# Expert tiles of a mixture-of-experts stage taken in pairs, with the results folded by a product instead of transposed and added

## The chip, the cores and the metric

One core of one Trainium2 chip. The metric is the device time of one execution in microseconds (us); the kernel before has a median of 809.62 us over 3 runs (809.58 to 811.24). TensorE is the matrix engine, VectorE (DVE) and ScalarE (ACT) work elementwise, GpSimd (POOL) does here the scatters, SyncE (SP) issues loads. Matmuls read SBUF and write PSUM, which has eight banks of 128 x 512 fp32.

## The reference, cut to what matters

`x` is 32 x 64 x 16 x 16, that is 8192 tokens of 64 channels. A depthwise convolution and a hashed attention block come first; the change doesn't touch them. Then each token goes to two of eight experts, each a gated network with 682 hidden units:

```python
probs = softmax(flat @ router_w.T)
topk_probs, topk_idx = top_k(probs, 2)
topk_probs = topk_probs / (sum(topk_probs) + 1e-9)
h1 = einsum('nc,ehc->neh', flat, w1)
h3 = einsum('nc,ehc->neh', flat, w3)
y = einsum('neh,ech->nec', silu(h1) * h3, w2)
out = einsum('ne,nec->nc', gates, y)
```

The kernel computes only the two experts chosen for a token. All of it is in fp32.

## The kernel before, in words

**First part (to about 430 us).** Eight groups of four images run through a software pipeline. At its end each token's normalised row, its gate and its destination are scattered to HBM (`expert_rows`), sorted by expert, and a small schedule says for each of NT = 71 tiles of MT = 256 rows which expert and which rows it has. An expert row holds the 64 values twice, then the gate, then the place of the result.

**The expert loop (437 to 783 us)** is what the change touches. A tile goes through these steps, each on the engine named; the order of each engine's work is written out by hand, and semaphores tie the engines together.

- SP, `load_weights(t)` (L382 to L386): 576 KB of the expert's weights into one of 4 slots, after `down` of tile t-4. `load_rows(t)` (L388 to L392): 256 rows into one of 8 slots of `xin`, after the scatter of tile t-8, which reads that slot. SP issues them in turn (L402 to L405): weights of t, rows of t+3, weights of t+1. A wait for one holds up all that follow.
- TensorE, `turn_rows(t)` (L731): two 128x128 transposes of the rows into the PSUM view `xt_ps`, which shares a bank with `h1_ps[0]`. ScalarE copies it into `xs` (`store_xs`, L917).
- TensorE, `up(t, q)`, q = 0 to 2 (L738): 8 products of 64 x 128 weights with 256 tokens; w1 lies on the upper 64 partitions and w3 on the lower. Each q fills a bank `h1_ps[q]` and a bank `h3_ps[q]`.
- ScalarE takes silu of `h1_ps[q]` (L933), VectorE multiplies it with `h3_ps[q]` into `units` (`gated`, L1250 to L1256).
- TensorE, `down(t)` (L752): 12 products of 128 x 64 weights with 256 tokens, accumulated in one bank, even chunks on partitions 0 to 63 and odd ones on 64 to 127. So the bank holds two half sums. ScalarE copies it into `ysb` (`store_results`, L922).
- TensorE, `turn_results(t)` (L762): two 128x128 transposes of `ysb` into the other half of the bank. A row then has the two half sums side by side.
- VectorE, `gate_out(t)` (L1258 to L1268): copies one half, adds the other, multiplies by the gate into `yout`: three passes over 128x128.
- GpSimd, L514 to L522: two indirect scatters of 128 rows into `expert_results`.

TensorE's order (L768 to L780) is up(t), turn_rows(t+1), turn_results(t-2), down(t-1). ScalarE's (L927 to L938) is three silus, store_xs(t+1), store_results(t-1). VectorE's (L1270 to L1276) is three gated units, gate_out(t-2).

**After the loop** SP and ScalarE read both results of every token back, VectorE adds them and the residual, and ScalarE stores the output.

Of the kernel before, what the change touches and what calls it, by code (L numbers as in the profile page):

```python
# [6 lines left out]
P = 128  # L7
B, C, HH, WW = 32, 64, 16, 16
# [14 lines left out]
MT = 256  # L23
REG = T + MT
NT = (2 * T + NE * (MT - 1)) // MT
ROW = 2 * C + 2
ROW_SLOTS = 3
DUMP = 2 * T
# [14 lines left out]

CONSTS = dict(ident=P, pair_mean=P, before=P, ones=P, descend=BUCKETS, head_of=HEADS, v_mask=2 * C,
              v_heads=2 * HEADS, region=NE * NJ, scan_keep=NE * (NJ + 1), k_rows=T // MT, tile_no=1, tile_at=1,
              pad=2 * ROW, q_one=1, k_one=1)
SMALLS = dict(bias2=1, g1=1, b1=1, g2=1, b2=1, fc1_bias0=2, proj=C + M + 2 * C, fc1=DFF, fc2=2 * C, fc2_bias=C,
              router=NE)

# [13 lines left out]
def hybrid_block(nc, x, consts, smalls, weights, out):  # L63
    with ExitStack() as ctx:
# [15 lines left out]
        def const_of(name, p=P):  # L80
            return const[0:p, CONST_AT[name][0]:CONST_AT[name][1]]
# [14 lines left out]
        k_rows = const_of("k_rows")  # L96
        tile_no = const_of("tile_no")
        tile_at = const_of("tile_at")
        pad = const_of("pad").rearrange("p (h w) -> p h w", h=2)
        bias2 = small_of("bias2")  # L100
        g1 = small_of("g1", C)
# [108 lines left out]

        xin = sb("xin", [P, X_SLOTS, 2, ROW])
        wbuf = sb("wbuf", [P, W_SLOTS, CH * P + CH * C])
        xs = sb("xs", [P, 2, MT])
        silu = sb("silu", [P, NU, 512])
        units = sb("units", [P, 2, NU, 512])
        ysb = sb("ysb", [P, 2, MT])
        ysum = sb("ysum", [P, 2, 2, C])
        yout = sb("yout", [P, X_SLOTS, 2, C])
        res = srow[:, :, :, :, :].rearrange("p g k j w -> p (g k j w)")[:, 0:RES_SLOTS * 2 * NJ * C]\
            .rearrange("p (b k j c) -> p b k j c", b=RES_SLOTS, k=2, c=C)  # L220
# [23 lines left out]

        h1_ps = [bk12[:, 0, :], bk12[:, 1, :], bk34[:, 0, :]]
        h3_ps = [bk34[:, 1, :], bk5[:, :], bk6]
        xt_ps = h1_ps[0][:, 0:MT]
        yt_banks = [bk0, bk7]

        waited = sem("waited")  # L250
        consts_loaded = sem("consts_loaded")
# [93 lines left out]
        down_done = sem("down_done")  # L345
        ysb_ready = sem("ysb_ready")
        y_turned = sem("y_turned")
        ysum_ready = sem("ysum_ready")
        yout_ready = sem("yout_ready")
        res_loaded = [sem(f"res_loaded{b}") for b in range(RES_SLOTS)]  # L350
        t3_sum = sem("t3_sum")
# [64 lines left out]
        def _(pool):  # L416
# [95 lines left out]
            pipeline(iteration)  # L512

            for t in range(NT):  # L514
                pool.wait_ge(yout_ready, t + 1)
                pool.sem_inc(waited, 1)
                for h in range(2):
                    g.indirect_dma_start(  # L518
                        results[:, :],
                        bass.IndirectOffsetOnAxis(ap=xin[:, t % X_SLOTS, h, ROW - 1:ROW].bitcast(U32), axis=0),  # L520
                        yout[:, t % X_SLOTS, h, :], None, bounds_check=DUMP - 1, oob_is_err=False)\
                        .then_inc(y_scattered[t % X_SLOTS], 16)  # L522

        @block.tensor
        def _(pe):
# [204 lines left out]

            def turn_rows(t):  # L731
                pe.wait_ge(xin_loaded[t % X_SLOTS], 16 * (t // X_SLOTS + 1))
                wait(pe, silu_ready, NU * (t - 1) + 1)
                for h in range(2):
                    last = turn(xt_ps[:, h * P:(h + 1) * P], xin[:, t % X_SLOTS, h, 0:2 * C], ident)  # L735
                last.then_inc(xt_turned, 1)

            def up(t, q):  # L738
                if q == 0:
                    pe.wait_ge(xs_ready, t + 1)  # L740
                    pe.wait_ge(w_loaded[t % W_SLOTS], 16 * (t // W_SLOTS + 1))
                wait(pe, unit_ready, NU * (t - 1) + q + 1)
                for ch in range(2):
                    at = (2 * q + ch) * P
                    for half, bank in ((0, h1_ps[q]), (1, h3_ps[q])):
                        part = slice(half * C, (half + 1) * C)
                        last = mm(bank[:, ch * MT:(ch + 1) * MT], wbuf[part, t % W_SLOTS, at:at + P],  # L747
                                  xs[part, t % 2, :], start=True, stop=True)
                        if ch == 1:
                            last.then_inc((h1_ready, h3_ready)[half], 1)  # L750

            def down(t):  # L752
                wait(pe, yout_ready, t - 1)
                pe.wait_ge(unit_ready, NU * (t + 1))
                for q in range(NU):
                    for ch in range(2):
                        at = W2_AT + (2 * q + ch) * C
                        last = mm(yt_banks[t % 2][ch * C:(ch + 1) * C, 0:MT], wbuf[:, t % W_SLOTS, at:at + C],  # L758
                                  units[:, t % 2, q, ch * MT:(ch + 1) * MT], start=q == 0, stop=q == NU - 1)
                last.then_inc(down_done, 1)  # L760

            def turn_results(t):  # L762
                pe.wait_ge(ysb_ready, t + 1)
                for h in range(2):
                    last = turn(yt_banks[t % 2][:, MT + h * P:MT + (h + 1) * P], ysb[:, t % 2, h * P:(h + 1) * P], ident)  # L765
                last.then_inc(y_turned, 1)

            turn_rows(0)  # L768
            for t in range(NT):
                for q in range(NU):  # L770
                    up(t, q)
                if t + 1 < NT:
                    turn_rows(t + 1)
                if t > 1:
                    turn_results(t - 2)
                if t > 0:
                    down(t - 1)
            turn_results(NT - 2)
            down(NT - 1)
            turn_results(NT - 1)  # L780

        @block.scalar
        def _(act):
# [130 lines left out]
            for e in range(NE // 2, NE):  # L914
                write_pad(act, act.value_load(pad_row[0:1, e:e + 1], min_val=0, max_val=NE * REG - MT))

            def store_xs(t):  # L917
                act.wait_ge(xt_turned, t + 1)
                wait(act, h3_ready, NU * (t - 1))
                f(xs[:, t % 2, :], xt_ps, ACT.Copy).then_inc(xs_ready, 1)  # L920

            def store_results(t):  # L922
                act.wait_ge(down_done, t + 1)
                wait(act, y_turned, t - 1)
                f(ysb[:, t % 2, :], yt_banks[t % 2][:, 0:MT], ACT.Copy).then_inc(ysb_ready, 1)  # L925

            store_xs(0)  # L927
            for t in range(NT):
                for q in range(NU):
                    n = NU * t + q  # L930
                    act.wait_ge(h1_ready, n + 1)
                    wait(act, unit_ready, n - NU + 1)
                    f(silu[:, q, :], h1_ps[q], ACT.Silu).then_inc(silu_ready, 1)  # L933
                if t + 1 < NT:
                    store_xs(t + 1)
                if t > 0:
                    store_results(t - 1)
            store_results(NT - 1)  # L938

            for b in range(X_SLOTS):  # L940
                act.wait_ge(y_scattered[b], 32 * ((NT - b + X_SLOTS - 1) // X_SLOTS))
# [19 lines left out]
        def _(dve):  # L961
# [293 lines left out]
                    wait(dve, down_done, t - 1)  # L1255
                tt(units[:, t % 2, q, :], h3_ps[q], silu[:, q, :], ALU.mult).then_inc(unit_ready, 1)  # L1256

            def gate_out(t):  # L1258
                dve.wait_ge(y_turned, t + 1)
                halves = yt_banks[t % 2][:, MT:2 * MT].rearrange("p (h a c) -> p h a c", h=2, a=2)  # L1260
                v.tensor_copy(ysum[:, t % 2, :, :], halves[:, :, 0, :]).then_inc(ysum_ready, 1)
                dve.wait_ge(ysum_ready, 2 * t + 1)
                tt(ysum[:, t % 2, :, :], halves[:, :, 1, :], ysum[:, t % 2, :, :], ALU.add).then_inc(ysum_ready, 1)
                dve.wait_ge(ysum_ready, 2 * t + 2)
                dve.wait_ge(xin_loaded[t % X_SLOTS], 16 * (t // X_SLOTS + 1))
                wait(dve, y_scattered[t % X_SLOTS], 32 * (t // X_SLOTS))
                tt(yout[:, t % X_SLOTS, :, :], ysum[:, t % 2, :, :],  # L1267
                   wide(xin[:, t % X_SLOTS, :, 2 * C], C), ALU.mult).then_inc(yout_ready, 1)  # L1268

            for t in range(NT):  # L1270
                for q in range(NU):
                    gated(t, q)
                if t > 1:
                    gate_out(t - 2)
            gate_out(NT - 2)
            gate_out(NT - 1)  # L1276

            for i in range(NG):
                dve.wait_ge(res_loaded[i % RES_SLOTS], 32 * (i // RES_SLOTS + 1))
# [5 lines left out]


DVE_SETUP = 2


def wait(engine, semaphore, value):  # L1290
# [18 lines left out]
def constants():  # L1309
    import numpy as np  # L1310

    p = np.arange(P)[:, None]
    n = np.arange(P)[None, :]
    h = np.arange(HEADS)
    t = {name: np.zeros((P, wide), np.float32) for name, wide in CONSTS.items()}
    t["ident"][:] = p == n
    t["pair_mean"][:] = 0.5 * (p // 2 == n // 2)
    t["before"][:] = p < n
    t["ones"][:] = 1.0
    t["descend"][:] = BUCKETS - np.arange(BUCKETS)  # L1320
    t["head_of"][:] = (p // DH == h) | (p >= C)
    head = np.arange(2)[None, :, None] * 4 + p[:, :, None] // M
    t["v_mask"][:] = (head == np.arange(C)[None, None, :] // DH).reshape(P, -1)
    t["v_heads"][:] = (head == h[None, None, :]).reshape(P, -1)
    t["region"][:] = np.repeat(np.arange(NE) * REG, NJ)
    t["scan_keep"][:] = np.tile(np.arange(NJ + 1) > 0, NE)
    t["k_rows"][:] = np.arange(T // MT) * MT
    t["tile_no"][:] = p
    t["tile_at"][:] = p * MT
    pad = np.zeros((P, 2, ROW), np.float32)  # L1330
    pad[:, :, ROW - 1] = np.full((P, 2), DUMP, np.uint32).view(np.float32)
    t["pad"][:] = pad.reshape(P, -1)
    t["q_one"][C] = 1.0
    t["k_one"][C + 1] = 1.0
    return np.concatenate([t[name] for name in CONSTS], axis=1)

# [56 lines left out]
```

## Time and profile before

| | |
|---|---|
| median of 3 runs | 809.62 us (809.58 to 811.24) |
| span of the profiled execution | 809.8 us |
| TensorE busy, weight loads apart | 664.6 us (82%) |
| VectorE, ScalarE, GpSimd busy | 462.7, 354.0, 370.7 us |
| first `up` of the expert loop, first `up` of its last tile | 437.22, 775.10 us |
| results read back from | 789.75 us |

The profiled execution's own time is its span, 809.8 us. The profile is of one execution. Starts of instructions are recorded; ends of matmuls are modelled, so that matmuls seem to overlap. PE is TensorE's matmuls, PEld its weight loads. An entry in brackets says how long an engine was idle before an instruction and what released it. An SPq row is the issue of a transfer by SP, not the transfer.

### The profile page before, as it was taken

Reading aid. Unit: us, or ns where it says so; the run is one execution under the profiler, and the core shown is the slowest. Engines: PE = TensorE matmul, PEld = TensorE weight load, DVE = VectorE, ACT = ScalarE, POOL = GpSimd, SP = SyncE. Lnnn points to the kernel's source line nnn. Section 1 sums busy time; section 2 is a strip of 40 time slices with the busy share of each in tenths; the row PEclk is TensorE's granted clock in tenths of the full one; section 3 lists DMA queues with packets and bytes.
Section 4 is the critical chain, followed back from the end, with each engine's and each line's share of the span. In section 5 each row is a group of like instructions: output and inputs, shape, how many; then the busy total and the mean of one; then the engine's idle time right before and its main releaser. Section 6 shows DMA issues by size and latency. Waiting matters only on the chain.

```text
span 809.8 us, 13968 instructions
## 1 busy us (share of the span) xinstructions
PE 664.6 (82%) x4632; PEld 502.3 (62%) x4632; DVE 462.7 (57%) x1094; ACT 354.0 (44%) x693; POOL 370.7 (46%) x377
## 2 busy tenths in 40 slices
PE   2598989797989797886404999999999999999960
PEld 1476768586867576673303777777777777777740
DVE  2256677677777777633311565566655666555645
ACT  1142737373737373523202544555445554455520
POOL 2203241767676768726662233443334433344440
PEclk9665868677777878555556999999999999999985
DMA  2000000010101010101183455556555555555508
GB/s 82 2 14 1 14 0 15 16 51 17 50 18 37 18 37 17 47 7 40 36 194 96 136 168 158 155 157 164 175 169 160 155 160 161 174 167 167 171 9 311
DMA packets 46615, 75.47 MB, mean 93 GB/s; under 512 B 7488, under 2 KB 30048, under 8 KB 46544
## 3 DMA queue, kind: packets, MB, share of 16 engines
q1 hardware_dynamic: 34512, 57.12, 24.2%
q0 software_dynamic: 8640, 12.74, 4.8%
q10 hardware_dynamic: 3392, 4.73, 1.8%
q8 instruction: 37, 0.61, 0.3%
q14 instruction: 34, 0.28, 0.1%
HBM read 58.54 MB, written 16.47 MB: 93 GB/s over the span
## 4 chain that ended last, share of the span: by engine, by line
PE 49%; POOL 23%; issue 17%; DVE 6%; DMA 3%; ACT 1%; POOLq 0%; SPq 0%; ACTq 0%; DVEq 0%
PE bk L747 25%; POOL expert_rows L496 15%; PE bk L758 12%; PE bk L735 3%; POOL rr L451 3%; PE bk L765 2%; DMA srow<-expert_results 2%; POOL r L462 2%; PE bk L553 1%; POOL x2t L480 1%; POOL r L457 1%; PE bk L577 1%; PE bk L570 1%; PE bk L638 1%; DMA small<-in_smalls 1%
## 5 line engine op out<-in xcount | busy, mean ns | idle before, releaser
L1256 DVE TENSOR_TENSOR units<-bk,silu 128x512 f32<-128x512 f32 x213 | 147.4, 692 | 164.7 <-ACT silu L933 164.7
L518 POOL DMA_INDIRECT expert_results<-yout,xin x142 | 139.5, 983 | 217.2 <-DVE yout L1267 190.4
L747 PE MATMUL bk<-xs,wbuf 64*128 64x256 f32 x1704 | 204.4, 386 | 1.2 <-ACT xs L920 1.1
L747 PEld LDWEIGHTS bk<-xs,wbuf 64*128 64x128 f32 x1704 | 160.0, 188 | 44.3 <-issue 26.7
L933 ACT ACTIVATE silu<-bk 128x512 f32<-128x512 f32 x213 | 127.2, 597 | 86.1 <-PE bk L747 86.1
L496 POOL DMA_INDIRECT expert_rows<-srow,pos x128 | 131.3, 1026 | 44.2 <-issue 38.0
L758 PE MATMUL bk<-units,wbuf 128*64 128x256 f32 x852 | 107.6, 388 | 0.0
L758 PEld LDWEIGHTS bk<-units,wbuf 128*64 128x64 f32 x852 | 54.8, 136 | 32.4 <-issue 11.7
L925 ACT ACTIVATE ysb<-bk 128x256 f32<-128x256 f32 x71 | 27.3, 384 | 84.2 <-PE bk L758 84.2
L451 POOL TENSOR_TENSOR rr<-vare,c_mhalf 128x16 f32<-128x16 f32 x8 | 23.4, 2923 | 79.3 <-DVE vare L1036 79.3
L735 PE MATMUL bk<-const,xin 128*128 128x128 f32 x142 | 31.3, 302 | 29.2 <-DMA xin<-expert_rows 29.2
L735 PEld LDWEIGHTS bk<-const,xin 128*128 128x128 f32 x142 | 14.3, 141 | 52.5 <-issue 52.5
L920 ACT ACTIVATE xs<-bk 128x256 f32<-128x256 f32 x71 | 26.9, 378 | 34.7 <-PE bk L735 34.7
L638 PEld LDWEIGHTS bk<-vblk,prob_t 128*128 128x128 f32 x256 | 34.8, 218 | 6.6 <-ACT prob_t L845 4.8
L665 PEld LDWEIGHTS bk<-small,hid 128*128 128x128 f32 x256 | 35.8, 227 | 1.8 <-ACT hid L861 1.8
L638 PE MATMUL bk<-vblk,prob_t 128*128 128x72 f32 x256 | 36.8, 305 | 0.0
L613 PE MATMUL bk<-kblk,qt 65*128 65x256 f32 x128 | 36.8, 425 | 0.0
L665 PE MATMUL bk<-small,hid 128*128 128x64 f32 x256 | 36.5, 311 | 0.2 <-ACT hid L861 0.2
L553 PE MATMUL bk<-const,hsum 128*128 128x128 f32 x192 | 36.5, 344 | 0.0
L1086 DVE TENSOR_REDUCE smax<-bk 128x16 f32<-128x512 f32 x32 | 21.8, 681 | 25.7 <-PE bk L613 25.5
L838 ACT ACTIVATE prob<-ssub 128x512 f32<-128x512 f32 x32 | 19.4, 626 | 37.3 <-DVE ssub L1088 37.2
L553 PEld LDWEIGHTS bk<-const,hsum 128*128 128x128 f32 x192 | 34.2, 262 | 0.0
(184 smaller groups left out, 981.5 us busy)
## 6 DMA issues: line engine op xcount, KB each, us to landing
wbuf<-in_weights SPq DMA_DIRECT2D x71, 576.0 KB, 4.0
xin<-expert_rows SPq DMA_DIRECT2D x71, 130.0 KB, 2.3
expert_results<-yout,xin POOLq DMA_INDIRECT x142, 2.8
xg<-in_x SPq DMA_DIRECT2D x8, 256.0 KB, 2.8
expert_rows<-srow,pos POOLq DMA_INDIRECT x128, 2.4
srow<-expert_results SPq DMA_DIRECT2D x8, 256.0 KB, 5.6
srow<-expert_results ACTq DMA_DIRECT2D x8, 256.0 KB, 6.4
out<-hid ACTq DMA_DIRECT2D x8, 256.0 KB, 5.8
```

Source lines behind the costliest of these rows:

```text
L451: g.tensor_tensor(rr[:, :, :].rearrange("p a j -> p (a j)"), vare1[:, :, :].rearrange("p a j -> p (a j)"), c_mhalf[:, :], ALU.pow).then_in ...
L496: g.indirect_dma_start(rows[0:NE * REG, :], bass.IndirectOffsetOnAxis(ap=pos[:, d, k, j:j + 1], axis=0), srow[:, d % ROW_SLOTS, k, j, :], ...
L518: g.indirect_dma_start(results[:, :], bass.IndirectOffsetOnAxis(ap=xin[:, t % X_SLOTS, h, ROW - 1:ROW].bitcast(U32), axis=0), yout[:, t % ...
L553: last = mm(o, hsum[:, s, h0 + dy:h0 + dy + 8, :], ident, start=False, stop=dy == 2)
L613: last = mm(bk12[:, p % 2, bp * 256:(bp + 1) * 256], qt[:, j * P:(j + 1) * P], kblk[:, m, :, :].rearrange("c h m -> c (h m)"), start=True, ...
L638: last = mm(av_ps[:, 2 * (p % 2) + bp, :], prob_t[:, p % 2, 2 * bp + ch, :], vblk[:, m, ch, :], start=ch == 0, stop=ch == 1)
L665: last = mm(y_ps[:, 2 * q + par, :], hid[:, a, par, q * P:(q + 1) * P], fc2_s[:, a, :], start=a == 0, stop=a == 1)
L735: last = turn(xt_ps[:, h * P:(h + 1) * P], xin[:, t % X_SLOTS, h, 0:2 * C], ident)
L747: last = mm(bank[:, ch * MT:(ch + 1) * MT], wbuf[part, t % W_SLOTS, at:at + P], xs[part, t % 2, :], start=True, stop=True)
L758: last = mm(yt_banks[t % 2][ch * C:(ch + 1) * C, 0:MT], wbuf[:, t % W_SLOTS, at:at + C], units[:, t % 2, q, ch * MT:(ch + 1) * MT], start= ...
L933: f(silu[:, q, :], h1_ps[q], ACT.Silu).then_inc(silu_ready, 1)
L1256: tt(units[:, t % 2, q, :], h3_ps[q], silu[:, q, :], ALU.mult).then_inc(unit_ready, 1)
```

## The change

The loop runs over NPAIR = 36 pairs of tiles; the last pair has tile 70 alone. TensorE's order for pair i is: up of both tiles (six groups of 8 products), row turns of pair i+1, folds of pair i-1, then down of both tiles of pair i. `xs` holds both tiles of a pair side by side and is filled by one copy of 512 columns; the turned rows fill the whole bank `h1_ps[0]`.

The result turn becomes `fold_results`: a product whose stationary operand is `ysb` (128 x 128) and whose moving operand is a constant 128 x 64 matrix `fold`, two 64 x 64 identities on top of each other. It turns the results and adds the two half sums at once. The folds of a pair fill 4 x 64 = 256 columns of the bank `h3_ps[0]`. `gate_out` is then one multiplication over 128 x 256 for a pair, from PSUM to `yout`. `down` accumulates in a bank of its own for each tile of a pair. SP's order and the slots stay; GpSimd's scatters of both tiles wait for the pair's `gate_out`.

```diff
@@ constants
-              pad=2 * ROW, q_one=1, k_one=1)
+              pad=2 * ROW, q_one=1, k_one=1, fold=C)
+    t["fold"][:] = p % C == np.arange(C)[None, :]
@@ tiles
-        xs = sb("xs", [P, 2, MT])
+        xs = sb("xs", [P, 2 * MT])
-        xt_ps = h1_ps[0][:, 0:MT]
-        yt_banks = [bk0, bk7]
+        xt_ps = h1_ps[0]
+        fold_ps = h3_ps[0]
+        y_banks = [bk0, bk7]
@@ GpSimd
             for t in range(NT):
-                pool.wait_ge(yout_ready, t + 1)
+                pool.wait_ge(yout_ready, t // 2 + 1)
@@ TensorE
             def turn_rows(t):
                 pe.wait_ge(xin_loaded[t % X_SLOTS], 16 * (t // X_SLOTS + 1))
-                wait(pe, silu_ready, NU * (t - 1) + 1)
+                wait(pe, silu_ready, NU * (t - 1 - t % 2) + 1)
...
             def up(t, q):
                 if q == 0:
-                    pe.wait_ge(xs_ready, t + 1)
+                    pe.wait_ge(xs_ready, t // 2 + 1)
                     pe.wait_ge(w_loaded[t % W_SLOTS], 16 * (t // W_SLOTS + 1))
+                    wait(pe, yout_ready, t // 2 - 1)
                 wait(pe, unit_ready, NU * (t - 1) + q + 1)
...
             def down(t):
-                wait(pe, yout_ready, t - 1)
+                wait(pe, ysb_ready, t - 1)
                 pe.wait_ge(unit_ready, NU * (t + 1))
...
-            def turn_results(t):
+            def fold_results(t):
                 pe.wait_ge(ysb_ready, t + 1)
+                wait(pe, yout_ready, t // 2)
+                wait(pe, unit_ready, NU * min(2 * (t // 2) + 3, NT - 1) + 1)
                 for h in range(2):
-                    last = turn(yt_banks[t % 2][:, MT + h * P:MT + (h + 1) * P], ysb[:, t % 2, h * P:(h + 1) * P], ident)
+                    at = (2 * (t % 2) + h) * C
+                    last = mm(fold_ps[:, at:at + C], ysb[:, t % 2, h * P:(h + 1) * P], fold, start=True, stop=True)
                 last.then_inc(y_turned, 1)
 
-            turn_rows(0)
-            for t in range(NT):
-                for q in range(NU):
-                    up(t, q)
-                if t + 1 < NT:
-                    turn_rows(t + 1)
-                if t > 1:
-                    turn_results(t - 2)
-                if t > 0:
-                    down(t - 1)
-            turn_results(NT - 2)
-            down(NT - 1)
-            turn_results(NT - 1)
+            for t in range(2):
+                turn_rows(t)
+            for i in range(NPAIR):
+                for t in pair(i):
+                    for q in range(NU):
+                        up(t, q)
+                if i + 1 < NPAIR:
+                    for t in pair(i + 1):
+                        turn_rows(t)
+                if i > 0:
+                    for t in pair(i - 1):
+                        fold_results(t)
+                for t in pair(i):
+                    down(t)
+            for t in pair(NPAIR - 1):
+                fold_results(t)
@@ ScalarE
+            def store_xs(i):
+                n = len(pair(i))
+                act.wait_ge(xt_turned, 2 * i + n)
+                wait(act, h3_ready, NU * 2 * i)
+                f(xs[:, 0:n * MT], xt_ps[:, 0:n * MT], ACT.Copy).then_inc(xs_ready, 1)
...
+            for i in range(NPAIR):
+                for t in pair(i):
+                    for q in range(NU):
...
+                if i + 1 < NPAIR:
+                    store_xs(i + 1)
+                for t in pair(i):
+                    store_results(t)
@@ VectorE
+            def gate_out(i):
+                n = len(pair(i))
+                dve.wait_ge(y_turned, 2 * i + n)
+                for t in pair(i):
+                    dve.wait_ge(xin_loaded[t % X_SLOTS], 16 * (t // X_SLOTS + 1))
+                    wait(dve, y_scattered[t % X_SLOTS], 32 * (t // X_SLOTS))
+                at = 2 * i % X_SLOTS
+                tt(yout[:, at:at + n, :, :], fold_ps[:, 0:2 * n * C].rearrange("p (t h c) -> p t h c", t=n, h=2),
+                   xin[:, at:at + n, :, 2 * C].unsqueeze(3).broadcast_to([P, n, 2, C]), ALU.mult).then_inc(yout_ready, 1)
+
+            for i in range(NPAIR):
+                for t in pair(i):
+                    for q in range(NU):
+                        gated(t, q)
+                if i > 0:
+                    gate_out(i - 1)
+            gate_out(NPAIR - 1)
+
+def pair(i):
+    return range(2 * i, min(2 * i + 2, NT))
```

## Rows read from the trace of the kernel before

**Rows 1.** Busy time by stretch: stretch, length, engines (instructions), TensorE clock, DMA.

```profile
600.00:620.00 20.00, 20.00 (x168) 14.16 (x168) 12.13 (x26) 10.01 (x21) 7.86 (x8) 1.00 0.57 167
```

**Rows 2.** Timeline of TensorE over one tile: start, us, line, operation, [idle before].

```profile
606.08 2.86 PE L747 MATMUL bk<-xs,wbuf 64*128 64x256 f32 x24
...
608.88 0.44 PE L735 MATMUL bk<-const,xin 128*128 128x128 f32 x2
...
609.15 0.38 PE L765 MATMUL bk<-const,ysb 128*128 128x128 f32 x2
...
609.46 1.52 PE L758 MATMUL bk<-units,wbuf 128*64 128x256 f32 x12
...
610.91 2.86 PE L747 MATMUL bk<-xs,wbuf 64*128 64x256 f32 x24
```

**Rows 3.** Products of `up` and `down`: count, ns least/median/most, first and last start.

```profile
L747 PE MATMUL bk<-xs,wbuf x1704: 376/376/790, 437.2 to 777.6; 64*128 64x256 f32 x190
...
L758 PE MATMUL bk<-units,wbuf x852: 379/379/431, 445.5 to 781.8; 128*64 128x256 f32 x171
```

**Rows 4.** Waits of SP's queue, 460 to 760 us: total, times, longest.

```profile
SPq L390 <- DMA expert_results<-yout,xin: 154.2, 56, 5.2
```

**Rows 5.** Timeline of TensorE in the first part: fc2, then transposes.

```profile
99.59 3.73 PE L665 MATMUL bk<-small,hid 128*128 128x64 f32 x32
103.15 1.04 PE L625 MATMUL bk<-const,prob 128*128 128x128 f32 x8
```

**Rows 6.** Timeline of VectorE and GpSimd beside the tile of rows 2.

```profile
607.88 0.69 DVE L1256 TENSOR_TENSOR units<-bk,silu 128x512 f32<-128x512 f32 x1 [1.55 <-ACT silu L933]
...
610.85 0.29 DVE L1267 TENSOR_TENSOR yout<-ysum,xin 128x128 f32<-128x128 f32 x1
...
612.00 0.98 POOL L518 DMA_INDIRECT expert_results<-yout,xin  x1 [2.55 <-DVE yout L1267]
...
613.28 0.98 POOL L518 DMA_INDIRECT expert_results<-yout,xin  x1 [0.30 <-issue]
```

**Rows 7.** Timeline of the loop's head: row loads, first copy, first and third `up`.

```profile
433.90 6.58 SPq L391 DMA_DIRECT2D xin<-expert_rows  x6
...
436.78 0.38 ACT L920 ACTIVATE xs<-bk 128x256 f32<-128x256 f32 x1 [34.69 <-PE bk L735]
...
437.22 4.13 PE L747 MATMUL bk<-xs,wbuf 64*128 64x256 f32 x24 [0.47 <-ACT xs L920]
...
446.92 2.86 PE L747 MATMUL bk<-xs,wbuf 64*128 64x256 f32 x24
```

**Rows 8.** Timeline of a tile's second scatter and of SP's issues after it.

```profile
574.70 0.98 POOL L518 DMA_INDIRECT expert_results<-yout,xin  x1 [0.30 <-issue]
...
580.66 0.38 SPq L391 DMA_DIRECT2D xin<-expert_rows  x1
...
603.64 0.98 POOL L518 DMA_INDIRECT expert_results<-yout,xin  x1 [0.30 <-issue]
...
608.38 0.38 SPq L391 DMA_DIRECT2D xin<-expert_rows  x1
...
609.54 0.35 SPq L385 DMA_DIRECT2D wbuf<-in_weights  x1
...
622.93 0.98 POOL L518 DMA_INDIRECT expert_results<-yout,xin  x1 [0.30 <-issue]
...
625.88 0.38 SPq L391 DMA_DIRECT2D xin<-expert_rows  x1
```

**Rows 9.** Issue to landing, 460 to 760 us: weights first, then the scatters.

```profile
DMA to landing us min/median/max: 3.4/4.0/5.4
...
DMA to landing us min/median/max: 2.1/2.9/5.2
```

**Rows 10.** Timeline of the loop's end: last `up`, read-back.

```profile
775.10 2.86 PE L747 MATMUL bk<-xs,wbuf 64*128 64x256 f32 x24
...
789.75 9.04 SPq L412 DMA_DIRECT2D srow<-expert_results  x8
```

More of the change, by code:

```diff
@@ L25 @@
 NT = (2 * T + NE * (MT - 1)) // MT
+NPAIR = (NT + 1) // 2
 ROW = 2 * C + 2
@@ L98, in hybrid_block @@
         tile_at = const_of("tile_at")
+        fold = const_of("fold")
         pad = const_of("pad").rearrange("p (h w) -> p h w", h=2)
@@ L216, in hybrid_block @@
         ysb = sb("ysb", [P, 2, MT])
-        ysum = sb("ysum", [P, 2, 2, C])
         yout = sb("yout", [P, X_SLOTS, 2, C])
@@ L347, in hybrid_block @@
         y_turned = sem("y_turned")
-        ysum_ready = sem("ysum_ready")
         yout_ready = sem("yout_ready")
@@ L732, in turn_rows @@
                 pe.wait_ge(xin_loaded[t % X_SLOTS], 16 * (t // X_SLOTS + 1))
-                wait(pe, silu_ready, NU * (t - 1) + 1)
+                wait(pe, silu_ready, NU * (t - 1 - t % 2) + 1)
                 for h in range(2):
-                    last = turn(xt_ps[:, h * P:(h + 1) * P], xin[:, t % X_SLOTS, h, 0:2 * C], ident)
+                    last = turn(xt_ps[:, (2 * (t % 2) + h) * P:(2 * (t % 2) + h + 1) * P], xin[:, t % X_SLOTS, h, 0:2 * C], ident)
                 last.then_inc(xt_turned, 1)
@@ L747, in up @@
                         last = mm(bank[:, ch * MT:(ch + 1) * MT], wbuf[part, t % W_SLOTS, at:at + P],
-                                  xs[part, t % 2, :], start=True, stop=True)
+                                  xs[part, t % 2 * MT:(t % 2 + 1) * MT], start=True, stop=True)
                         if ch == 1:
@@ L757, in down @@
                         at = W2_AT + (2 * q + ch) * C
-                        last = mm(yt_banks[t % 2][ch * C:(ch + 1) * C, 0:MT], wbuf[:, t % W_SLOTS, at:at + C],
+                        last = mm(y_banks[t % 2][ch * C:(ch + 1) * C, 0:MT], wbuf[:, t % W_SLOTS, at:at + C],
                                   units[:, t % 2, q, ch * MT:(ch + 1) * MT], start=q == 0, stop=q == NU - 1)
                 last.then_inc(down_done, 1)
-            def turn_results(t):
+            def fold_results(t):
                 pe.wait_ge(ysb_ready, t + 1)
+                wait(pe, yout_ready, t // 2)
+                wait(pe, unit_ready, NU * min(2 * (t // 2) + 3, NT - 1) + 1)
                 for h in range(2):
-                    last = turn(yt_banks[t % 2][:, MT + h * P:MT + (h + 1) * P], ysb[:, t % 2, h * P:(h + 1) * P], ident)
+                    at = (2 * (t % 2) + h) * C
+                    last = mm(fold_ps[:, at:at + C], ysb[:, t % 2, h * P:(h + 1) * P], fold, start=True, stop=True)
                 last.then_inc(y_turned, 1)
-            turn_rows(0)
-            for t in range(NT):
-                for q in range(NU):
-                    up(t, q)
-                if t + 1 < NT:
-                    turn_rows(t + 1)
-                if t > 1:
-                    turn_results(t - 2)
-                if t > 0:
-                    down(t - 1)
-            turn_results(NT - 2)
-            down(NT - 1)
-            turn_results(NT - 1)
+            for t in range(2):
[14 more added lines that the diff above has]
+                fold_results(t)
         @block.scalar
@@ L915, in _ @@
                 write_pad(act, act.value_load(pad_row[0:1, e:e + 1], min_val=0, max_val=NE * REG - MT))
[L917 to L920, printed above, removed]
+            def store_xs(i):
[3 more added lines that the diff above has]
+                f(xs[:, 0:n * MT], xt_ps[:, 0:n * MT], ACT.Copy).then_inc(xs_ready, 1)
             def store_results(t):
@@ L924, in store_results @@
                 wait(act, y_turned, t - 1)
-                f(ysb[:, t % 2, :], yt_banks[t % 2][:, 0:MT], ACT.Copy).then_inc(ysb_ready, 1)
+                f(ysb[:, t % 2, :], y_banks[t % 2][:, 0:MT], ACT.Copy).then_inc(ysb_ready, 1)
             store_xs(0)
[L928 to L938, printed above, removed]
+            for i in range(NPAIR):
+                for t in pair(i):
+                    for q in range(NU):
+                        n = NU * t + q
+                        act.wait_ge(h1_ready, n + 1)
+                        wait(act, unit_ready, n - NU + 1)
+                        f(silu[:, q, :], h1_ps[q], ACT.Silu).then_inc(silu_ready, 1)
+                if i + 1 < NPAIR:
+                    store_xs(i + 1)
+                for t in pair(i):
+                    store_results(t)
             for b in range(X_SLOTS):
@@ L1256, in gated @@
                 tt(units[:, t % 2, q, :], h3_ps[q], silu[:, q, :], ALU.mult).then_inc(unit_ready, 1)
[L1258 to L1276, printed above, removed]
+            def gate_out(i):
[14 more added lines that the diff above has]
+            gate_out(NPAIR - 1)
             for i in range(NG):
```

## The prediction

> **What bounds the kernel now.** The views were read from the coarse to the fine. The chain of work that ended last gives the time between 437 and 783 us to the lines of the expert loop, nearly all TensorE's; the change touches that loop alone (and 64 columns of constants). The busy time by stretch shows TensorE at 20.00 of 20 us, clock 1.00, so 2.4 GHz, while VectorE has 12.1, ScalarE 10.0 and GpSimd 7.9 [rows 1]. Then the timeline of one tile, from start to start, since ends of matmuls are modelled [rows 2]: `up` (24 products) begins at 606.08, the two row turns at 608.88, the two result turns at 609.15, `down` (12 products) at 609.46, the next `up` at 610.91. A tile takes 4.83 us.
>
> Inside `up` the starts are (2.86 - 0.376)/23 = 0.108 us apart (a product is shown with 0.376, the median of its line [rows 3]), inside `down` (1.52 - 0.379)/11 = 0.104; two turns begin (0.38 - 0.27) = 0.11 apart, a turn being shown with about 0.27. So the last `up` product starts at 608.56, and the turn only 0.32 later; from the last `down` product (610.60) to the next `up` it is 0.31; from turns to `down` 0.20; from turn to turn of the other kind 0.16. The reader should see that a change of the kind of product costs about 0.2 us over the pace inside a kind, four kinds to a tile.
>
> The other thing to see is off TensorE. SP issues in order: rows of t+3, weights of t+1, rows of t+4. The rows wait for the scatter of the tile eight earlier, 154 us in 56 waits, up to 5.2 [rows 4]. Weights queue behind that wait. Today it costs nothing; by how much, is worked out below.
>
> **The change, for a pair of tiles.** Call S the start of a pair's first `up`.
> 1. Kinds of product: 48 `up` products, 4 row turns, 4 folds, 24 `down` products, so four changes of kind where two tiles have eight. 47 x 0.108 + 0.32 + 3 x 0.11 + 0.16 + 3 x 0.112 + 0.20 + 23 x 0.104 + 0.31 = 9.12 us, against 2 x 4.83 = 9.65 measured: 0.53 less.
> 2. Folds. A fold is a true fp32 product with 128 stationary columns and 64 moving ones, in place of a transpose. This kernel has such products in fc2: 32 in 3.73 us, so (3.73 - 0.27)/31 = 0.112 each; and 8 transposes right behind them, (1.04 - 0.27)/7 = 0.11 [rows 5]. The fold costs nothing more; the transposes of this stretch keep the pace of those in the expert loop, so the clock is the same. The Trainium skill (TensorE: Matmul & The Clock Gate, Terms) calls transpose mode four times faster for fp32; by that the sum would be 843 (rival C), and the rows of fc2 disagree.
> 3. New waits on TensorE. Second `up` needs the first tile's products gated bank by bank. The first gated unit starts at S + 1.80 and takes 0.69 [rows 6], so it is done at S + 2.49; a release takes 0.06 (ScalarE ends at 437.16, TensorE starts at 437.22 [rows 7]): S + 2.55. TensorE gets there at S + 24 x 0.108 = 2.59. The product just fits, but its weight load, which runs ahead, does not. Bounds: 0, and 0.2 us a pair, the price of a change of kind, where the loads are not hidden either; nothing is gained by a wait. I take the middle, 0.1, so 9.22. The second `down` needs the last gated unit: units come 8 x 0.108 = 0.86 apart, the sixth ends at S + 1.80 + 5 x 0.86 + 0.69 = 6.8; `down` gets there at S + 7.7. Next `up` writes the bank of the folds and waits for the gating of the pair before, done at S + 7.3 of the earlier pair: 1.8 us to spare. Turns wait for a silu done 0.6 us before.
> 4. VectorE: three passes of 0.29 a tile become one of 128x256 a pair, between 0.29 (128x128) and 0.69 (128x512), linear 0.43. VectorE is not the bound; gain 0. It moves the output: folds end at S + 6.5, the pass waits in order for the sixth gated unit and ends at S + 7.3.
> 5. ScalarE: one copy of 512 columns for two of 256, ready at about S + 6.8, needed at S + 9.1: 0. The result copies now follow each `down`; the next silu is due 1.1 us after the next `up` starts, and a copy takes 0.4: 0.
> 6. GpSimd and SP. Today the first scatter starts 0.86 after yout (611.14 to 612.00) and the second 1.28 later [rows 6]. Now both tiles' yout come at once, so four follow each other: starts S + 8.15, 9.44, 10.7, 12.0. Nobody waits for GpSimd but SP. From the start of a tile's second scatter to SP's issue of the rows it frees I read D = 2.95 (622.93 to 625.88), 4.74 (603.64 to 608.38) and, the longest found, 5.96 (574.70 to 580.66); weights are issued 1.16 later (608.38 to 609.54) [rows 8] and land after 4.0 (3.4 to 5.4) [rows 9]. So the weights of the pair two ahead land at S + 9.44 + D + 1.16 + 4.0 = S + 14.6 + D, and are needed at S + 2 x 9.12 = 18.2. D may be 3.6. Today the same sum is 7.2 + D + 5.16 against 4 x 4.83 = 19.3: D may be 6.9, which no row reaches. The change eats 3.3 us of that margin. Which D will hold? My guess is that the long ones have weights in flight beside them. If so, by the schedule above the earlier pair's second weight load is issued at about S + 7 and lands at S + 11 to 11.7; the second scatter sends its data from S + 10.4, so it meets the tail of it only: D about 3.2 to 3.7. A longer pair would thin the traffic. So the loop lies near the limit, and I take it as costing nothing on the mean, with 9.4 as its upper bound (D = 4.2).
> The page DMA: Bandwidth & Descriptors of the Trainium skill (the fit under its fixed cost) gives 2.0 us plus bytes over 436 GB/s for a software DMA. A scatter of 32 KB would land in 2.1 us by it, D near 2.9, and this limit would never bite; the trace has 2.1 as the least, 2.9 as the median and 5.2 as the most [rows 9].
> 7. Head. The first `up` now waits for the rows of tile 1 too. Six row loads are issued in 6.58 us, 1.24 apart; so `up` begins near 438.5 in place of 437.22 [rows 7]. The low clock of the first products cost it 1.27 (4.13 for 2.86); I take 1.7, since TensorE has done less before it. 438.5 + 47 x 0.108 + 1.7 + 0.32 + 0.33 + 0.2 + 2.4 + 0.31 puts pair 1 at 448.9, where tile 2 began at 446.92: +2.0 us.
> 8. Tail. Tile 70 stands alone. Today SP reads the results back 14.65 us after its `up` (775.10 to 789.75), by six scatters at the end that wait in GpSimd's line [rows 10]. Now six scatters again, the first at S + 5.5: 5.5 + 6 x 1.29 + 1.0 = S + 14.3: -0.35.
> 9. Constants grow from about 0.56 to 0.59 MB, 0.1 us at most: 0.
>
> **The sum.** Pair 35 starts at 448.9 + 34 x 9.22 = 762.4, against 775.10: -12.7; tail -0.35; -13.0 in all. The profiled execution's span is 809.8, the median 809.62, 0.02% apart. 809.6 - 13.0 = 796.6. With 9.12: 793.2. With 9.40: 802.7. About 0.2%, 1.6 us, is what a measurement here can tell from no change.
>
> **Rivals.**
> A. The forecast, 0.70: TensorE stays the bound, 9.12 to 9.4 us a pair. For: full busy time now, other engines at 60% or less, the 0.3 us at each change of kind.
> B. Weights late, the rival on the slow side: SP issues them behind the rows, rows behind the later, bunched scatters. The pair takes (14.6 + D)/2. It decides from D = 3.6; at D = 4.4 it is 9.5 and the time 806; the gain is gone at 9.60, D = 4.6; at D = 5 it is 9.8 and the time 816; at 5.96, 832. For it: two of the three D read are over 4.6. Against: the guess of step 6, by which the second scatter meets the end of a weight transfer only. Partly so (gain left, up to 808): 0.12. Equal: 0.03. Slower, about 816: 0.11.
> C. The fold is dear: if a true fp32 product is four passes of the array where a transpose is one, it takes 4 x 0.11 = 0.44, and 142 of them add 142 x 0.33 = 47 us: 843. The fc2 rows stand against it: 0.02. (It is the Trainium skill's rule of step 2.)
> D. The change does not do what it says: at each place where a change of kind goes, TensorE waits for a gated unit instead. Should the second `up` wait 0.5 us a pair, the time is 809. That step 3 leaves only 0.04 us of room is for it, the bound of 0.2 there against: 0.02.
>
> **How the numbers follow.** The likeliest case is A, 796.6. Chances: faster A and the partial B, 0.82; same 0.03 + 0.02 = 0.05; slower 0.11 + 0.02 = 0.13. The range goes down to 790.5 (9.05 a pair, should one of the changes of kind left be cheaper than today, and pair 1 a microsecond earlier) and up to 806.5 (B with D = 4.4).
>
> **What would show it.** In steady state: 48 `up` products in one run of starts 0.108 apart, at the most a gap of 0.1 at the 25th; folds 0.11 apart; pairs 9.2 apart; TensorE with next to no idle on a DMA. Rival B would show as TensorE idle before `up`, released by DMA wbuf, and D over 4. Rival C as folds 0.4 apart. The forecast is wrong if pairs are over 9.45 or under 9.05 apart, or if the head costs over 3 us.

## The result, and the profile after

The changed kernel takes 814.06 us (median of 20 runs, 810.9 to 817.71) against 810.15 us of the kernel before in the same runs (808.24 to 813.04): a ratio of 1.0043, 95% interval 1.003 to 1.0056. It is slower by 3.5 us by that ratio, 3.9 by the medians, where 13 us less was forecast. The profiled execution has a span of 811.5 us and a time of 813.63. In every run with both numbers on record the time is 1.7 to 2.2 us over the span; the text ahead of the prediction takes the profiled execution of the kernel before to have its span, 809.8 us, as its time, which leaves these 2 us out. The difference that was forecast doesn't hang on it.

TensorE's timeline of one pair in steady state, kernel after (start, us, operation):

```profile
603.12 5.49 PE L749 MATMUL bk<-xs,wbuf 64*128 64x256 f32 x48
...
608.54 0.66 PE L736 MATMUL bk<-const,xin 128*128 128x128 f32 x4
...
609.03 1.00 PE L770 MATMUL bk<-const,ysb 128*128 128x64 f32 x8
...
609.97 2.81 PE L760 MATMUL bk<-units,wbuf 128*64 128x256 f32 x24
...
612.71 5.49 PE L749 MATMUL bk<-xs,wbuf 64*128 64x256 f32 x48
```

A pair takes 9.59 us, against 9.65 for two tiles before [rows 2]. Start to start: `up` 5.42, turns 0.49, folds 0.94, `down` 2.74. The line of the folds is the one to look at. The code calls for four products in a pair and the row says x8. The view of that line says the same for the whole run: 142 calls, 284 matmuls. The first fence is of the kernel after (count, ns least/median/most, first and last start), the second has the result turns of the kernel before, 142 calls and 142 matmuls:

```profile
L770 PEld LDWEIGHTS bk<-const,ysb x284: 186/192/192, 454.5 to 783.8; 128*128 128x128 f32 x142
L770 PE MATMUL bk<-const,ysb x284: 222/275/323, 454.6 to 783.9; 128*128 128x64 f32 x142
```

```profile
L765 PEld LDWEIGHTS bk<-const,ysb x142: 137/141/143, 449.9 to 782.7; 128*128 128x128 f32 x142
L765 PE MATMUL bk<-const,ysb x142: 272/273/329, 450.0 to 782.8; 128*128 128x128 f32 x142
```

The stretch that answers to [rows 1] shows TensorE full as before and VectorE relieved, 9.83 of 20 us for 12.13:

```profile
600.00:620.00 20.00, 20.00 (x176) 15.94 (x177) 9.83 (x16) 10.14 (x19) 7.86 (x8) 1.00 0.59 183
```

Not every pair is steady. Here a pair's weights are late, those of its first tile a little and those of its second more (timeline of GpSimd, SP's issues and TensorE, kernel after):

```profile
525.43 0.98 POOL L519 DMA_INDIRECT expert_results<-yout,xin  x1 [0.30 <-issue]
...
530.18 0.38 SPq L392 DMA_DIRECT2D xin<-expert_rows  x1
531.35 0.35 SPq L386 DMA_DIRECT2D wbuf<-in_weights  x1
...
533.67 0.35 SPq L386 DMA_DIRECT2D wbuf<-in_weights  x1
...
535.32 2.86 PE L749 MATMUL bk<-xs,wbuf 64*128 64x256 f32 x24
...
538.39 2.86 PE L749 MATMUL bk<-xs,wbuf 64*128 64x256 f32 x24 [0.21 <-DMA wbuf<-in_weights]
```

The second scatter of a tile starts at 525.43, SP issues the rows it frees 4.75 us later, the weights behind them at 531.35 and 533.67. The pair before began at 525.50, so the first `up` comes 9.82 after it in place of 9.59, 0.23 late. The second starts at 538.39, 3.07 after the first, in place of 2.69, its distance in 30 of the 34 full pairs from pair 1 on (a little more than 24 x 0.109, since the starts inside `up` come in twos, some 0.01 to 0.04 us apart, and from two to two it is 0.216). The views of waits of TensorE and of SP, 460 to 770 us, kernel after:

```profile
PE bk L749 <- DMA wbuf<-in_weights: 0.9, 2, 0.7
```

```profile
SPq L391 <- DMA expert_results<-yout,xin: 165.7, 43, 9.6
```

SP's longest wait went from 5.2 [rows 4] to 9.6 us, but that one stands where the loop fills, from 450.9 to 461.2 us; from 470 us on the longest is 5.9. The sum of TensorE's waits by name (0.9) understates the cost, since idle time counts only from the modelled end of the last matmul (535.32 + 2.86 = 538.18, so 0.21 above, where by the starts 0.38 was lost); by starts, pairs 1 to 35 span 777.17 - 448.72 = 328.45 us where 33 x 9.59 and a last 9.38 make 325.85. So 2.6 us of this trace are weights that came late.

More than half of them follow one late scatter. GpSimd then idles 1.97 us in place of 0.30 before it, put down to "issue"; what that is, no run shows. Timeline of GpSimd and of TensorE, kernel after:

```profile
729.65 0.98 POOL L519 DMA_INDIRECT expert_results<-yout,xin  x1 [1.97 <-issue]
...
741.65 2.86 PE L749 MATMUL bk<-xs,wbuf 64*128 64x256 f32 x24 [0.68 <-DMA wbuf<-in_weights]
```

The two pairs around it take 10.07 and 10.50 us in place of 9.59, 1.4 us of the 2.6. Such a pause stands in the other traces too: in experiment 3 at 727.22, where no pair is longer for it, and in the kernel before at 725.89, where the weights of tile 62, issued at 732.91, make a tile of 5.01 us (731.49 to 736.50) in place of 4.83.

**The balance of the two traces**, from SP's first row load to the read-back: before 433.90 to 789.75, 355.85; after 432.95 to 791.30, 358.35; 2.5 more. Head, to the start of tile 2: 13.0, then 15.8: +2.75. Tiles 2 to 70: 328.2, then 328.45: +0.3, made of -2.3 (pairs at 9.59 and a last of 9.38) and +2.6 (late weights). Tail: 14.65, then 14.13: -0.5. The medians stand 3.9 apart; the other 1.4 is within the scatter of single runs.

### The profile page after: what moved, and what is told of

It reads as the page before. It is cut to its first block, busy times and chain, and to the rows that moved or that the text cites. A ratio compares the mean times of both kernels' runs of the same rounds, so it can differ in the third digit from the quotient of the medians.

```text
span 811.5 us, 14139 instructions
## 1 busy us (share of the span) xinstructions
PE 664.7 (82%) x4774; PEld 531.7 (66%) x4774; DVE 422.1 (52%) x917; ACT 355.6 (44%) x658; POOL 371.0 (46%) x377
## 4 chain that ended last, share of the span: by engine, by line
PE 47%; POOL 23%; issue 17%; DVE 6%; DMA 5%; ACT 1%; SPq 1%; POOLq 0%; ACTq 0%; DVEq 0%
PE bk L749 23%; POOL expert_rows L497 15%; PE bk L760 11%; PE bk L770 3%; POOL rr L452 3%; PE bk L736 3%; POOL r L463 2%; PE bk L554 1%; DMA wbuf<-in_weights 1%; POOL x2t L481 1%; POOL r L458 1%; PE bk L578 1%; PE bk L571 1%; DMA out<-hid 1%; DMA srow<-expert_results 1%
## 5 line engine op out<-in xcount | busy, mean ns | idle before, releaser
L749 PE MATMUL bk<-xs,wbuf 64*128 64x256 f32 x1704 | 198.0, 385 | 2.3 <-DMA wbuf<-in_weights 0.9
L749 PEld LDWEIGHTS bk<-xs,wbuf 64*128 64x128 f32 x1704 | 167.5, 188 | 32.5 <-issue 16.6
L760 PE MATMUL bk<-units,wbuf 128*64 128x256 f32 x852 | 99.9, 383 | 0.5 <-DVE units L1265 0.5
L760 PEld LDWEIGHTS bk<-units,wbuf 128*64 128x64 f32 x852 | 58.3, 137 | 28.3 <-issue 0.6
L736 PE MATMUL bk<-const,xin 128*128 128x128 f32 x142 | 24.1, 291 | 29.9 <-DMA xin<-expert_rows 29.9
L929 ACT ACTIVATE xs<-bk 128x512 f32<-128x512 f32 (+1 forms) x36 | 21.3, 591 | 36.9 <-PE bk L736 36.0
L666 PEld LDWEIGHTS bk<-small,hid 128*128 128x128 f32 x256 | 35.8, 227 | 1.8 <-ACT hid L869 1.8
L666 PE MATMUL bk<-small,hid 128*128 128x64 f32 x256 | 36.5, 311 | 0.2 <-ACT hid L869 0.2
L770 PE MATMUL bk<-const,ysb 128*128 128x64 f32 x284 | 35.9, 269 | 0.5 <-ACT ysb L934 0.5
L770 PEld LDWEIGHTS bk<-const,ysb 128*128 128x128 f32 x284 | 34.5, 192 | 1.3 <-ACT ysb L934 0.9
```

The source lines that it names most:

```text
L666: last = mm(y_ps[:, 2 * q + par, :], hid[:, a, par, q * P:(q + 1) * P], fc2_s[:, a, :], start=a == 0, stop=a == 1)
L736: last = turn(xt_ps[:, (2 * (t % 2) + h) * P:(2 * (t % 2) + h + 1) * P], xin[:, t % X_SLOTS, h, 0:2 * C], ident)
L760: last = mm(y_banks[t % 2][ch * C:(ch + 1) * C, 0:MT], wbuf[:, t % W_SLOTS, at:at + C], units[:, t % 2, q, ch * MT:(ch + 1) * MT], start=q ...
L770: last = mm(fold_ps[:, at:at + C], ysb[:, t % 2, h * P:(h + 1) * P], fold, start=True, stop=True)
```

## The experiments

Theory F: a plain fp32 product goes to TensorE as two matmuls of about 0.11 us and a transpose as one, so the folds cost 0.4 us a pair, and the pairing itself saves what was forecast. Theory W: weights are late behind the bunched scatters, through SP's order. The main rival, K: changes of kind are not what pairs save. All variants with pairs are edits of the changed kernel. Each run stood beside runs of the kernel before on the same chip; 811.28 us (first four) and 811.19 us (last four) were its medians.

**1. Pairs, with transposes in place of folds.**

```diff
...
-                    at = (2 * (t % 2) + h) * C
-                    last = mm(fold_ps[:, at:at + C], ysb[:, t % 2, h * P:(h + 1) * P], fold, start=True, stop=True)
+                    at = (2 * (t % 2) + h) * P
+                    last = turn(fold_ps[:, at:at + P], ysb[:, t % 2, h * P:(h + 1) * P], ident)
@@ gate_out
+                halves = fold_ps[:, 0:2 * n * P].rearrange("p (h a c) -> p h a c", h=2 * n, a=2)
+                v.tensor_copy(ysum[:, 0:2 * n, :], halves[:, :, 0, :]).then_inc(ysum_ready, 1)
+                dve.wait_ge(ysum_ready, 2 * i + 1)
+                tt(ysum[:, 0:2 * n, :], halves[:, :, 1, :], ysum[:, 0:2 * n, :], ALU.add).then_inc(ysum_ready, 1)
+                dve.wait_ge(ysum_ready, 2 * i + 2)
...
```

The part left out makes the tile `ysum` and its semaphore, and multiplies `ysum` by the gate in place of the folds.

> Pairs as in the change, but the results turned by transposes and the halves added by VectorE as before (three passes over 128x256). Theory F (a fold takes two matmuls of 0.112 us, a transpose one, and the pairing itself works): TensorE's work of a pair falls from 9.59 to 9.14 us. VectorE's three passes put the scatters 0.85 us later, so the weights of the pair two ahead land at S + 15.45 + D, with D about 3.5 as in the kernel after, which allows 9.48 a pair: 809 to 811 us, with TensorE waiting for wbuf in most pairs. Rival K (changes of kind are not what pairs save, and the fold costs nothing): pairs stay at 9.59 or more, 814 us or more. Rival N (weights never late for long): 9.14 a pair, 798 us.

Measured: 818.99 us, ratio 1.011 (1.007 to 1.015), slower than both kernels. TensorE's work fell as Theory F says; the weights ate it all. Timeline of TensorE and of SP's weight issues:

```profile
601.51 0.35 SPq L388 DMA_DIRECT2D wbuf<-in_weights  x1
...
602.80 2.86 PE L751 MATMUL bk<-xs,wbuf 64*128 64x256 f32 x24
...
605.81 2.86 PE L751 MATMUL bk<-xs,wbuf 64*128 64x256 f32 x24
...
611.23 0.35 SPq L388 DMA_DIRECT2D wbuf<-in_weights  x1
...
612.36 2.86 PE L751 MATMUL bk<-xs,wbuf 64*128 64x256 f32 x24
...
615.80 2.86 PE L751 MATMUL bk<-xs,wbuf 64*128 64x256 f32 x24 [0.58 <-DVE units L1267]
```

The second `up` comes 3.01 and 3.44 after the first, in place of 2.69. At 615.80 the view names VectorE as the releaser; but the gated unit that is waited for ends at 614.85 (614.16 + 0.69). The weights issued at 611.23 have a landing of their own in the view of transfers, 4.5 us later, at 615.7:

```profile
wbuf<-in_weights SPq DMA_DIRECT2D x1, 576.0 KB, 4.5
```

So this wait is put down to the wrong engine, and is one for weights. Pairs 1 to 35 span 780.68 - 446.80 = 333.9 us; experiment 7, in which no pair waits, has 312.15 for them: 22 us of waiting, 15 before the second `up` of a pair and 7 before the first. Expected was 809 to 811; the sign of the mechanism was right, its size was not.

**2. The same, with SP's rows two tiles ahead of the weights in place of three.** No weight load then stands behind the newest scatter.

```diff
-            for t in range(X_SLOTS - 2):
+            for t in range(X_SLOTS - 3):
                 load_rows(t)
...
-                if t + X_SLOTS - 1 - W_SLOTS < NT:
-                    load_rows(t + X_SLOTS - 1 - W_SLOTS)
+                if t + X_SLOTS - 2 - W_SLOTS < NT:
+                    load_rows(t + X_SLOTS - 2 - W_SLOTS)
```

> The same, and SP loads rows two tiles ahead of the weights in place of three, so that no weight load stands behind a late scatter. Theory F: 9.14 us a pair, no wait for wbuf, 814 - 15.3 - 2.5 = 796 us. Rival K: 811 to 814 us, 9.59 a pair.

Measured: 801.13 us, ratio 0.9871 (0.9847 to 0.9894). 18 us less than experiment 1, by the order of SP's loads alone. 796 was expected. A pair without a wait takes 9.19 us where 9.14 was expected, 1.7 us in 34; and pairs 1 to 35 take 764.66 - 449.54 = 315.1, 3.0 over the 312.15 of experiment 7. Two waits are put down to wbuf, 2.0 us together, so the order with rows two ahead doesn't end them all.

**3. The kernel of the change with that order of loads.** The same edit on the fold.

> The kernel of the change, with SP's rows two tiles ahead of the weights. Theory W (of the distance to the kernel before, 2.5 us are weights late now and then): every pair 9.59, no wait for wbuf, 811.5 us, about the time of before. Rival: the rows, not the weights, come late or nothing changes, 814 us.

Measured: 810.23 us, ratio 0.9991 (0.9974 to 1.0008), no wait for wbuf, and pairs 1 to 35 in 773.35 - 447.50 = 325.85 us, to the hundredth the 33 x 9.59 + 9.38 without a wait. The interval does not touch that of the change (1.003 to 1.0056). So late weights are most or all of what makes the change slower than before. Theory W holds, with one reserve: by the times the order of loads is worth 4 us here, by the trace 2.6, and experiment 6 leaves room for some 1 us that has nothing to do with pairs.

**4. Tile by tile, with the fold.** The kernel before, with only the product and VectorE's single pass (its edit is left out).

```diff
-                    last = turn(yt_banks[t % 2][:, MT + h * P:MT + (h + 1) * P], ysb[:, t % 2, h * P:(h + 1) * P], ident)
+                    last = mm(yt_banks[t % 2][:, MT + h * C:MT + (h + 1) * C], ysb[:, t % 2, h * P:(h + 1) * P], fold,
+                              start=True, stop=True)
...
```

> The kernel before, tile by tile, with the fold in place of the result transposes and of the two VectorE passes. Theory F: a tile takes 4.83 + 2 x 0.112 = 5.05 us, 810.2 + 71 x 0.224 = 826 us. Rival K (the fold costs what a transpose does): 810 us.

Measured: 822.13 us, ratio 1.0135 (1.0106 to 1.0164). TensorE's timeline of one tile, to be laid beside [rows 2]:

```profile
601.32 2.86 PE L748 MATMUL bk<-xs,wbuf 64*128 64x256 f32 x24
604.12 0.44 PE L736 MATMUL bk<-const,xin 128*128 128x128 f32 x2
604.39 0.56 PE L766 MATMUL bk<-const,ysb 128*128 128x64 f32 x4
604.88 1.52 PE L759 MATMUL bk<-units,wbuf 128*64 128x256 f32 x12
606.32 0.92 PE L748 MATMUL bk<-xs,wbuf 64*128 64x256 f32 x6
```

From the fold to `down` it is 0.49 in place of 0.31: a tile takes 5.00 us, 0.18 more, where 0.22 and 826 us were expected. From tile 2 to tile 70 this trace has 339.9 us against 328.2 before, 11.7 more, and behind the last `up` 0.7 less; 11 were measured. The fold alone is a loss.

**5. Plain product or stacked identity?** Experiment 2 with the result turns as plain products with the full identity, 128 moving columns; not one other instruction differs.

```diff
-                    last = turn(fold_ps[:, at:at + P], ysb[:, t % 2, h * P:(h + 1) * P], ident)
+                    last = mm(fold_ps[:, at:at + P], ysb[:, t % 2, h * P:(h + 1) * P], ident, start=True, stop=True)
```

> As pair_turn_rows2, but the four result turns of a pair are plain products with the full identity (128 moving columns) in place of transposes. Nothing else differs: same columns, same three VectorE passes, same SP order. Theory F (a plain fp32 product goes as two matmuls where a transpose goes as one, whatever its columns): 8 matmuls in place of 4, a pair 9.19 + 0.4 = 9.59 to 9.63 us, 801.1 + 14 = 815 us. Rival C (it was the stacked identity, or its 64 columns): 9.19 a pair, 801 us.

Measured: 814.08 us, ratio 1.0034 (1.0018 to 1.0051), 13 us over experiment 2. Pairs take 9.65 us. Its timeline, and that of experiment 7 (transposes) under it:

```profile
610.25 0.66 PE L738 MATMUL bk<-const,xin 128*128 128x128 f32 x4
610.74 1.06 PE L772 MATMUL bk<-const,ysb 128*128 128x128 f32 x8
611.73 2.81 PE L762 MATMUL bk<-units,wbuf 128*64 128x256 f32 x24
```

```profile
611.51 0.66 PE L738 MATMUL bk<-const,xin 128*128 128x128 f32 x4
612.00 0.60 PE L772 MATMUL bk<-const,ysb 128*128 128x128 f32 x4
612.53 2.81 PE L762 MATMUL bk<-units,wbuf 128*64 128x256 f32 x24
```

x8 and 0.99 us for the same four turns that are x4 and 0.53 as transposes. A call costs (1.06 - 0.275)/7 x 2 = 0.22 us as a plain product and (0.60 - 0.27)/3 = 0.11 as a transpose. It is the kind of product and not the shape: with half the columns the folds take 0.94, hardly less. No pair waits here, while experiment 2 has its 3.0 us of waits; so 34 x 0.46 = 15.6 less 3.0 is what the times should show, and 13 is what they show.

**6. The kernel before with rows two ahead.**

> The kernel before, with SP's rows two tiles ahead of the weights in place of three. Theory W (there the weights land long before they are needed): no change, 811 us. Rival (the order of the loads is worth something by itself): 1 us or more faster.

Measured: 809.67 us, ratio 0.9986 (0.9972 to 1.0001). That lies between theory (no change) and rival (1 us or more), and the interval, 2.3 us less to none, decides for neither; in the trace of the kernel before late weights cost 0.2 us, at one tile. The order of loads is worth 18 us to the pairs with transposes and 2 us at most to single tiles; it costs nothing there.

**7. Experiment 2 with rows one tile ahead of the weights** (`X_SLOTS - 4` and `X_SLOTS - 3 - W_SLOTS` in the edit of experiment 2).

> As pair_turn_rows2, rows one tile ahead of the weights. Theory W (what is left over 9.19 a pair, some 2.7 us in that trace with two waits for wbuf, is weights behind late scatters): no wait for wbuf, all pairs 9.19, 798.5 us. Rival (weights late for another reason, or rows now late): 801 us or more.

Measured: 798.26 us, ratio 0.9841 (0.9808 to 0.9874). All pairs are at 9.18 to 9.19: 449.90 to 762.05 is 312.15 us, the length without a wait (34 x 9.185, less 0.2 at the last). SP's waits, 450 to 765 us:

```profile
SPq L393 <- DMA expert_results<-yout,xin: 76.7, 32, 4.5
SPq L387 <- PE bk L762: 72.0, 32, 4.7
```

Half of SP's waiting is now for `down` to free a weight slot, and the weights that follow come in time: no wait of TensorE is put down to wbuf. The intervals of this run and of experiment 2 overlap; what tells them apart is the trace, 3.0 us in these pairs.

**8. The same, with the rows of tile 1 turned and copied behind the first tile's `up`** (ScalarE's copies and the waits that go with them are left out).

```diff
-            for t in range(2):
-                turn_rows(t)
+            turn_rows(0)
...
                     for q in range(NU):
                         up(t, q)
+                    if t == 0:
+                        turn_rows(1)
...
```

> As pair_turn_rows1, with the rows of tile 1 turned and copied behind the first tile's up, as the kernel before did it. The head of the pairs waits for rows 1 about 1.2 us; a change of kind and a copy come back, 0.5 us: 0.7 us less than pair_turn_rows1. If the head costs nothing: no difference.

Measured: 797.37 us, ratio 0.9832 (0.9797 to 0.9866). From the first row load to pair 1 it is 449.37 - 434.75 = 14.6 us, against 449.90 - 434.08 = 15.8 in experiment 7. The medians differ by 0.9, well inside both intervals: the trace shows the gain, the times cannot. It has the lowest time of all, 13 to 14 us under the kernel before.

## Why the prediction was wrong

**The step that failed is step 2**, the price of the folds. It priced a fold at one matmul of 0.112 us; a fold is two. The pace per matmul was right. The count was not: `down` is six calls and x12 [rows 2], `up` twelve calls and x24, fc2 sixteen calls (L663 to L666) and x32 [rows 5], while two turns are x2. Rows and code side by side had said that a plain fp32 product is two matmuls and a transpose one; the prediction read "24 products" and never counted the calls. (The same miscount stands ahead of the prediction: `up(t, q)` is not 8 products but 4, `down(t)` not 12 but 6, each two matmuls.) Four folds cost 0.94 us, start to start, in place of the 0.54 in the sum: 0.40 a pair, 14 us in 35 pairs. With it the forecast would have been 810.

The forecast for pair 1 to pair 35 was 34 x 9.22 = 313.5 us, and they took 328.45, 15.0 more. Four terms make it: folds 34 x 0.40 = 13.6; late weights 2.6; other steps of a pair, some hundredths each, 34 x 0.07 = 2.4; against them the wait of step 3, 3.4 in the forecast and not there, and 0.2 of the last pair.

Rival C had this in kind, with four matmuls for one in place of two, so 843. That rival B's slower case, about 816, lies near the 814 measured is chance: it has pairs of 9.8 us, all of it late weights, where they took 9.59, nearly all of it TensorE's own work. The Trainium skill (TensorE: Matmul & The Clock Gate, Terms) has transpose mode four times faster for fp32; in experiment 5 it is 0.99 against 0.53 us for four turns with the change of kind to `down`, and 0.22 against 0.11 for one call, so twice and not four times. The direction of the rule was right, and the rows that were held against it compared matmul with matmul, not call with call.

**Step 6 failed too**, hidden behind the first. It took late weights as costing nothing on the mean. At 9.59 us a pair they cost 2.6 us, which is what turned a tie into a loss; at 9.19, with transposes and the scatters 0.7 us later (0.85 was expected; S + 10.2 for the one of step 6, in pairs that don't wait, against S + 9.5), they cost 22 us, and the kernel is at 819. So a cheap turn alone does not bring the forecast time. Whether a fold as cheap as step 2 had it, with VectorE's single pass and so earlier scatters, would have stayed clear of the limit could not be tried. The mechanism stood as rival B: the place, the queue and the wait were right, the price for the pairs of experiment 1 was 809 to 811 and came out 8 us short. The formula looked only at the first tile's weights, needed at the pair's start. The second's are needed 2.69 us later, but SP issues them 2.3 us later at the least, and up to 3.5 in experiment 1, where they wait for the second tile's own scatter: 15 of the 22 us there are theirs, and 1.4 of the 2.6 in the kernel after.

The guess of D was too narrow also. By the starts in the trace of the kernel after, pairs 4 to 34, D of the first tile is 2.9 to 5.05, the median 3.6, and 15 of 31 are over the 3.6 that step 6 allows pairs of 9.12. So by an estimate from these numbers a cheap fold alone would have put about half the pairs at or over the limit, if D stayed as it is; how it moves with the length of a pair is not shown. What makes a scatter's D long was not tried.

The other steps:
- Step 1, changes of kind: `up` with its change 5.42 against 5.40, turns 0.49 against 0.49, `down` 2.74 against 2.70. Right; with transposes the pair takes 9.19, the sum had 9.12. Rival K falls: the pairing saves 0.46 us with transposes (9.65 to 9.19), and with folds 0.41 (two tiles at 5.00, 9.59). That is 0.12 for each of the four changes of kind that go. "About 0.2" was true of two of the four kinds of change only (0.32 - 0.11 and 0.31 - 0.10); the others had 0.05 and 0.09 over the pace, and the sum used each at its own size.
- Step 3, the second `up` waits 0.1: wrong, it waits nothing. 48 matmuls in one run, (5.49 - 0.376)/47 = 0.109 apart on the mean. The room is 0.14 us and not 0.04, since the starts come in twos and the 25th comes at S + 2.69. Rival D falls (by its own sum it stands at 810, not 809: 796.6 + 34 x 0.40).
- Steps 4 and 5, VectorE and ScalarE cost nothing: right for TensorE's pairs. But in experiment 1 VectorE's longer gating moves the scatters, and through them the weights.
- Step 7, head: +2.0 forecast, +2.75 measured.
- Step 8, tail: -0.35 forecast, -0.5 measured.

The four kernels of a two by two table show the sum in another way. The time of two tiles by kind of turn and by grouping: two single tiles with transposes 9.65, with folds 10.00; a pair with folds 9.59, with transposes 9.19. The change took what pairing gains and paid nearly all of it for folds.

## What to carry to other kernels

Before pricing an operation by a row, divide the row's count by the calls in the code: an fp32 product may be two matmuls where a transpose is one, and adding halves for free in a product is then no bargain if VectorE has room. When work is bunched, follow the slots it frees to the queue that waits for them, and ask what stands behind that wait: here the order of two kinds of loads was worth 18 us to pairs with transposes. A term found near its limit belongs in the sum with a price, not at zero.

## What was not expected of the hardware

The second `up` of a pair lost nothing, though by the sum of step 3 its wait ends just before it, after its weight load would have begun. In the pair that begins at 603.12 that load was held: it starts at 605.72, 0.34 us after the load before it, where the others follow 0.22 apart. The matmul still starts on pace, 0.216 after the 23rd. The stacked identity's 64 columns cost what 128 cost, 0.94 against 0.99 us for eight matmuls: halving the moving columns buys next to nothing. Each has a weight load of 128 columns before it, shown with 192 ns, in both; whether that sets the pace was not tried. A plain product's weight load is shown with 192 ns and a transpose's with 141, for the same 128 x 128 operand.
